# First stage of a graph network on one core: GpSimd's gathers held to four pairs ahead of VectorE's messages

## The chip, the cores and the metric

The kernel runs on one core of one Trainium2 chip. The metric is the device time of one execution in microseconds. The kernel before takes 1134.37 us, the median of three runs (1134.0 to 1136.73).

## What is computed

The reference is two graph layers over 3125 nodes and 53125 edges, the edges sorted by target node. The first layer gathers a row of `x` (256 floats) for every edge, scales it with the edge's weight, and sums over the edges of each target; the second layer adds a small network over 64 edge attributes to its messages and then puts each node through three dense layers (256 to 1024 to 1024 to 256) with layer norms.

```
messages = edge_val[:, None] * embeddings[edge_src]
neighbor_emb = segment_sum(messages, edge_dst)
out = leaky(embeddings @ W1.T + b1 + (neighbor_emb + neighbor_emb * embeddings) @ W2.T + b2)
x = layernorm(x + out / max(norm(out), eps))

e = relu(edge_attr @ ee_w1 + ee_b1) @ ee_w2 + ee_b2
h = (1 + eps) * x + segment_sum(x[src] + e, dst)
h = relu(ln(h @ w1 + b1)); h = relu(ln(h @ w2 + b2)); y = h @ w3 + b3
out = layernorm(x + relu(ln(x + y)))
```

## The kernel before, in words

Nodes are cut into 25 blocks of 128. Since edges are sorted, the edges of block q are close to a run of 17 tiles of 128 edges (the last block has 8). The tiles of a block are worked in 9 pairs: pairs 0 to 7 have two tiles, pair 8 has one (`PAIRS`). The kernel has two stages. The first stage makes, for each tile, a message in two parts (a high and a low half of float32), sums messages into target nodes by matmuls with one-hot matrices, and finishes the first layer for each block. It also sums the hidden activations of the edge network. The second stage gathers finished rows again and runs the three dense layers.

In the first stage each engine has its own written-out list of instructions, block after block; nothing but semaphores ties them together:

- GpSimd (`near_gathers`, L961) issues one indirect DMA a tile: 128 rows of `x` into `raw[:, j, :]`, where j is the tile's number in its block. `raw` has 17 places, so the gather of pair k of block q must wait until message pair k of block q-1 has read them. The semaphore `issued` counts gathers as GpSimd finishes issuing them; `gathered[j]` tells when the rows have landed.
- TensorE (`edge_layer`, L1102) multiplies the edge attributes of a pair into `ps_e` (three banks, so it waits for message pair k-2, L1106), sums tiles into `ps_sum` (`near_step`, L1118), and once a block transposes the finished sum `s_r` (`turn`, L1138), which increments `s_turned`.
- ScalarE (`highs`, L1652) writes the high halves of a pair: `raw` times the weight (L1658), and relu of `ps_e` (L1661), then increments `high`.
- VectorE (`near_block`) makes one-hots (`equal`, L216), then the low halves (L2162 and L2168); the last of them increments `message`, one for each pair. In step s of block b it works on message pair s+3 (LEAD = 3), counted on into block b+1. After the message it does a piece of the tail of an earlier block, and in step 1 `take_s` (L2173).
- SyncE loads attributes, weights and rows in its own order.

Two more ties matter. Before each pair VectorE runs `follow` (L2244), a wait that the pair's one-hot carries:

```
tiles = TILES * q + PAIRS[k][0] + 2 + AHEAD
dve.wait_ge(issued, tiles)
```

with AHEAD = 4 and TILES = 17. And from block FIRST_HELD = 4 on, GpSimd is held beyond what `raw` asks for: by HELD_PAIRS more messages, and before j = 2 by `s_turned`.

Of the kernel before, what the change touches and what calls it, by code (L numbers as in the profile page):

```python
# [48 lines left out]
assert LAST_TILES % 2 == 0  # L49
LEAD = 3  # L50
FIRST_HELD = 4
HELD_PAIRS = 3
AHEAD = 4
ENDING = 3
CHUNKS = [(0, 6), (6, 6), (12, 5)]
# [164 lines left out]
def is_last(b):  # L220

    return isinstance(b, int) and b == BLOCKS - 1
# [49 lines left out]
def gnn_program(nc, x, xT, src, dst, weight, attrT, w1T, w2T, bias01, bias02, eps_in, ee_w1, ee_b1row, ee_b1,  # L272
# [6 lines left out]
    with ExitStack() as keep:  # L279
# [29 lines left out]
        with ExitStack() as ca:  # L309
# [3 lines left out]
            def ma(name):  # L313
                return sem(name)
# [96 lines left out]
            s_turned = ma("s_turned")  # L411
# [513 lines left out]
        def _(pool):  # L925
# [35 lines left out]
            def near_gathers(q):  # L961

                for j in range(LAST_TILES if is_last(q) else TILES):
                    if j == 2 and q >= FIRST_HELD:
                        pool.wait_ge(s_turned, q - 1)
                    if j % 2 == 0:

                        pool.wait_ge(message, NP * (q - 1) + j // 2 + 1 + (HELD_PAIRS if q >= FIRST_HELD else 0))
                        pool.nop(nofuse=True)
                    pool.indirect_dma_start(  # L970
                        out=raw[:, j, :], out_offset=None, in_=x,
                        in_offset=bass.IndirectOffsetOnAxis(
                            ap=src_all[:, q * TILES + j:q * TILES + j + 1], axis=0),
                        engine_sem=issued,
                    ).then_inc(gathered[j], 16)

            def near_program(path):
                for q in range(1, BLOCKS):
                    near_gathers(q)
                second_near(path)  # L980
# [1846 lines left out]
```

## Time and profile before

| | us |
|---|---|
| median of three timed runs | 1134.37 |
| span of the profiled execution | 1477.5 |
| PE busy in it | 1201.4 |
| DVE busy | 976.8 |
| POOL busy | 812.9 |
| ACT busy | 686.1 |

For the profiled execution the span from the first to the last instruction is what is recorded; no device time of its own is given beside it. That span is 343 us longer than the median of the timed runs, so a row of the trace is not a share of the median. Engines: PE is TensorE's matmuls, PEld its weight loads, DVE VectorE, ACT ScalarE, POOL GpSimd, SP SyncE. "L970" is line 970 of the kernel. In brackets behind an instruction stands the idle time of its engine before it and what ended it; "issue" is time in which the engine waited for nothing that the profile shows, and "remote" is a release that the profile can't name. The ends of matmuls are modelled.

### The profile page before, as it was taken

To read this page: it belongs to the slowest core of one execution; us is meant where nothing else is said; L and a number is where in the kernel's file an instruction comes from. 1 tells how busy PE (TensorE), PEld (TensorE's weight loads), DVE (VectorE), ACT (ScalarE), POOL (GpSimd) and SP (SyncE) were. 2 spreads that over 40 slices of the span, in tenths; PEclk is the share of its full clock that TensorE was granted. 3 is DMA by queue.
4 is the path that set the end of the run, shared out by engine and by line. 5 is a ranking of instruction groups with operands and counts; after the bars stand their busy time and mean duration, and the time that the engine had idled before them with its cause. 6 is when DMAs were issued, how large, how long until landed. Compare 5 with 4: busy or idle time off the path is not lost.

```text
span 1477.5 us, 21215 instructions
## 1 busy us (share of the span) xinstructions
PE 1201.4 (81%) x5297; PEld 977.9 (66%) x5297; DVE 976.8 (66%) x2795; ACT 686.1 (46%) x1677; POOL 812.9 (55%) x840
## 2 busy tenths in 40 slices
PE   4788877787777887778777889888898898898897
PEld 3576666566666665566555677677776777776676
DVE  4767755667656775667666666666666676676575
ACT  2455644556445554455453443443533443443444
POOL 7555555455554555545645565566565566566530
PEclk9798887888878888788878899999999999999999
DMA  6345544445444444435565555656665566566540
GB/s 202 105 120 145 151 130 144 125 142 147 134 143 128 128 127 119 126 114 148 146 203 163 165 169 172 185 167 183 176 185 166 174 176 178 171 185 180 161 119 13
DMA packets 106088, 222.13 MB, mean 150 GB/s; under 512 B 20003, under 2 KB 57369, under 8 KB 106010
## 3 DMA queue, kind: packets, MB, share of 16 engines
q0 software_dynamic: 53408, 164.16, 39.1%
q1 hardware_dynamic: 52602, 57.11, 12.4%
q8 instruction: 27, 0.44, 0.1%
q14 instruction: 51, 0.42, 0.1%
HBM read 203.96 MB, written 17.23 MB: 150 GB/s over the span
## 4 chain that ended last, share of the span: by engine, by line
PE 34%; another core or an unknown queue 21%; DVE 16%; issue 16%; ACT 11%; DVEq 1%; DMA 1%; POOL 1%; ACTq 0%; POOLq 0%
PE ps_z L1386 8%; PE ps_e L1108 7%; PE ps_sum L1115 3%; PE ps_sum L1113 3%; ACT msg L1658 3%; ACT aF L1888 3%; PE ps_y L1386 3%; PE ps_s L1330 3%; DVE msg L2162 2%; DVE oh L216 2%; PE ps_tr L1455 2%; DVE msg L2168 2%; PE ps_w L1209 2%; ACT msg L1661 2%
## 5 line engine op out<-in xcount | busy, mean ns | idle before, releaser
L970 POOL DMA_INDIRECT raw<-in_x,src_all x399 | 385.6, 966 | 321.9 <-DVE msg L2168 177.2
L1031 POOL DMA_INDIRECT grow<-table_dram,src_all x401 | 392.7, 979 | 275.0 <-issue 115.1
L1108 PE MATMUL ps_e<-we,attr 65*128 65x256 f32 x832 | 251.1, 427 | 150.7 <-DVE msg L2168 127.0
L2162 DVE SCALAR_TENSOR_TENSOR msg<-raw,w_sb,msg 128x256 fp32r<-128x256 f32 x416 | 183.0, 478 | 242.5 <-issue 130.5
L1108 PEld LDWEIGHTS ps_e<-we,attr 65*128 65x128 f32 x832 | 171.5, 214 | 200.4 <-issue 173.3
L1661 ACT ACTIVATE msg<-ps_e 128x512 fp32r<-128x512 f32 (+1 forms) x220 | 124.3, 565 | 310.2 <-remote 221.1
L1113 PE MATMUL ps_sum<-msg,oh 128*128 128x512 f32 x464 | 255.8, 551 | 9.2 <-DVE msg L2168 8.8
L1386 PE MATMUL ps_z<-w_high,a 128*128 128x512 f32 x784 | 255.5, 395 | 7.7 <-issue 6.3
L216 DVE TENSOR_SCALAR oh<-lane,rel 128x128 fp32r<-128x128 f32 x871 | 208.1, 297 | 18.9 <-issue 15.7
L1115 PE MATMUL ps_sum<-msg,oh 128*128 128x512 f32 x464 | 210.1, 453 | 0.0
L1658 ACT ACTIVATE msg<-raw,w_sb 128x256 fp32r<-128x256 f32 x416 | 188.1, 498 | 10.3 <-issue 7.7
L1386 PEld LDWEIGHTS ps_z<-w_high,a 128*128 128x128 f32 x784 | 147.0, 188 | 40.1 <-issue 9.5
L1888 ACT ACTIVATE aF<-ps_tr,be,g 128x128 f32<-128x128 f32 x392 | 147.3, 464 | 53.7 <-PE ps_tr L1455 33.1
L1386 PE MATMUL ps_z<-w_low,a 128*128 128x512 f32 x392 | 153.4, 391 | 1.0 <-issue 0.8
L2168 DVE SCALAR_TENSOR_TENSOR msg<-ps_e,msg 128x512 fp32r<-128x512 f32 (+1 forms) x220 | 143.6, 653 | 0.0
L1455 PE MATMUL ps_tr<-ident,zn 128*128 128x128 f32 x400 | 64.3, 301 | 76.5 <-issue 38.8
L1113 PEld LDWEIGHTS ps_sum<-msg,oh 128*128 128x128 f32 x464 | 102.9, 222 | 34.0 <-issue 11.7
L1115 PEld LDWEIGHTS ps_sum<-msg,oh 128*128 128x128 f32 x464 | 104.1, 224 | 22.4
L1455 PEld LDWEIGHTS ps_tr<-ident,zn 128*128 128x128 f32 x400 | 50.1, 155 | 89.0 <-issue 88.4
L1330 PE MATMUL ps_s<-grow,oh 128*128 128x512 f32 x365 | 104.2, 429 | 0.4 <-issue 0.4
L1386 PE MATMUL ps_y<-w_high,a 128*128 128x256 f32 x400 | 89.6, 306 | 4.1 <-DVE a L2538 2.1
L1386 PEld LDWEIGHTS ps_z<-w_low,a 128*128 128x128 f32 x392 | 73.8, 188 | 18.6 <-issue 5.2
(189 smaller groups left out, 1591.6 us busy)
## 6 DMA issues: line engine op xcount, KB each, us to landing
attr<-in_attrT SPq DMA_DIRECT2D x50, 192.0 KB
raw<-in_x,src_all POOLq DMA_INDIRECT x416
grow<-table_dram,src_all POOLq DMA_INDIRECT x401
w_raw<-in_m_w SPq DMA_DIRECT2D x48, 128.0 KB
table_dram<-table SPq DMA_DIRECT2D x23, 256.0 KB
attr<-in_attrT SPq DMA_DIRECT2D x24, 160.0 KB
xs<-in_x SPq DMA_DIRECT2D x24, 128.0 KB
xTb<-in_xT SPq DMA_DIRECT2D x24, 128.0 KB
```

Of the source, the lines that this page charges most:

```text
L216: ins = dve.tensor_scalar(out_[:, i, :], lanes, which[:, i:i + 1], None, ALU.is_equal)
L970: pool.indirect_dma_start(out=raw[:, j, :], out_offset=None, in_=x, in_offset=bass.IndirectOffsetOnAxis(ap=src_all[:, q * TILES + j:q * TI ...
L1031: pool.indirect_dma_start(out=grow[:, j, :].bitcast(F32), out_offset=None, in_=table_dram, in_offset=bass.IndirectOffsetOnAxis(ap=src_all[ ...
L1108: mm = pe.matmul(ps_e[k % 3][:, (j - j0) * D:(j - j0 + 1) * D], attr[:, j * P:(j + 1) * P], we1[:, :], start=True, stop=True)
L1113: pe.matmul(ps_sum[bank][:, :], oh[:, slot, :], msg[:, j, 0, :], start=start, stop=False, skip_group_check=True)
L1115: return pe.matmul(ps_sum[bank][:, :], oh[:, slot, :], msg[:, j, 1, :], start=False, stop=stop, skip_group_check=True)
L1386: mm = pe.matmul(acc, left[a], right[b], start=False, stop=stop and a == 1, skip_group_check=True)
L1658: act.activation(msg[:, j, 0, 0:D], raw[:, j, :], ACT.Copy, scale=w_sb[:, tile_cols(n, j)])
L1661: act.activation(msg[:, j0:j0 + m, 0, D:2 * D], ps_e[k % 3][:, 0:m * D].rearrange("p (j d) -> p j d", d=D), ACT.Relu).then_inc(high, 1)
L1888: ins = act.activation(aF[layer][:, k, :], ps_tr[:, half, c * P:(c + 1) * P], ACT.Relu, bias=bb[:, k:k + 1], scale=gg[:, k:k + 1])
L2162: dve.scalar_tensor_tensor(msg[:, j, 1, 0:D], raw[:, j, :], w_sb[:, tile_cols(n, j)], msg[:, j, 0, 0:D].bitcast(F32), ALU.mult, ALU.subtract)
L2168: dve.scalar_tensor_tensor(msg[:, j0:j0 + m, 1, D:2 * D], ps_e[k % 3][:, 0:m * D].rearrange("p (j d) -> p j d", d=D), 0.0, msg[:, j0:j0 + ...
```

## The change

HELD_PAIRS goes from 3 to 5. From block 4 on the gather of pair k of block q waits for the messages up to pair k+5 of block q-1 instead of k+3, each counted on into block q where k+5 is over 8. The wait of the gather of tile 2 for the turned sum of block q-2 is taken out. Nothing else is changed.

```
-HELD_PAIRS = 3
+HELD_PAIRS = 5
...
             def near_gathers(q):

                 for j in range(LAST_TILES if is_last(q) else TILES):
-                    if j == 2 and q >= FIRST_HELD:
-                        pool.wait_ge(s_turned, q - 1)
                     if j % 2 == 0:

                         pool.wait_ge(message, NP * (q - 1) + j // 2 + 1 + (HELD_PAIRS if q >= FIRST_HELD else 0))
```

## Rows read from the trace of the kernel before

**Rows 1.** The page: busy shares, and groups of instructions with their idle time

```profile
PE 1201.4 (81%) x5297; PEld 977.9 (66%) x5297; DVE 976.8 (66%) x2795; ACT 686.1 (46%) x1677; POOL 812.9 (55%) x840
...
L970 POOL DMA_INDIRECT raw<-in_x,src_all x399 | 385.6, 966 | 321.9 <-DVE msg L2168 177.2
...
L2162 DVE SCALAR_TENSOR_TENSOR msg<-raw,w_sb,msg 128x256 fp32r<-128x256 f32 x416 | 183.0, 478 | 242.5 <-issue 130.5
```

**Rows 2.** Waits, whole span: us in total, times, longest

```profile
ACT msg L1661 <- remote: 221.1, 40, 7.9
...
PE ps_e L1108 <- DVE msg L2168: 127.0, 37, 7.6
...
ACT hT L1860 <- remote: 101.4, 21, 6.2
...
POOL raw L970 <- PE ps_t L1143: 36.5, 13, 3.9
...
DVE oh L216 <- issue: 15.7, 31, 1.2
```

**Rows 3.** Timeline of PE: start, duration, instruction

```profile
398.58 1.03 PE L1108 MATMUL ps_e<-we,attr 65*128 65x256 f32 x4
...
400.37 1.03 PE L1108 MATMUL ps_e<-we,attr 65*128 65x256 f32 x4
```

**Rows 4.** Timeline of ACT over the same stretch

```profile
404.04 0.60 ACT L1661 ACTIVATE msg<-ps_e 128x512 fp32r<-128x512 f32 x1 [3.87 <-PE ps_e L1108]
...
413.20 0.60 ACT L1661 ACTIVATE msg<-ps_e 128x512 fp32r<-128x512 f32 x1 [7.19 <-remote]
```

**Rows 5.** Timeline of POOL

```profile
393.28 0.94 POOL L970 DMA_INDIRECT raw<-in_x,src_all  x1 [2.94 <-PE ps_t L1143]
...
409.61 0.94 POOL L970 DMA_INDIRECT raw<-in_x,src_all  x1 [0.30 <-issue]
416.08 0.96 POOL L970 DMA_INDIRECT raw<-in_x,src_all  x1 [5.53 <-DVE msg L2168]
418.59 1.09 POOL L970 DMA_INDIRECT raw<-in_x,src_all  x1 [1.54 <-DVE msg L2168]
...
424.48 0.94 POOL L970 DMA_INDIRECT raw<-in_x,src_all  x1 [3.55 <-DVE msg L2168]
...
769.59 0.95 POOL L1031 DMA_INDIRECT grow<-table_dram,src_all  x1 [12.19 <-DMA table_dram<-w_high]
```

**Rows 6.** Timelines of DVE and, for turn's L1143, of PE

```profile
389.18 0.41 DVE L2181 SCALAR_TENSOR_TENSOR s_r<-xs,ps_sum 128x256 f32<-128x256 f32 x1
...
415.95 0.47 DVE L216 TENSOR_SCALAR oh<-lane,rel 128x128 fp32r<-128x128 f32 x2
...
417.13 0.68 DVE L2168 SCALAR_TENSOR_TENSOR msg<-ps_e,msg 128x512 fp32r<-128x512 f32 x1
...
419.78 0.41 DVE L2181 SCALAR_TENSOR_TENSOR s_r<-xs,ps_sum 128x256 f32<-128x256 f32 x1
...
421.63 0.68 DVE L2168 SCALAR_TENSOR_TENSOR msg<-ps_e,msg 128x512 fp32r<-128x512 f32 x1
...
422.62 0.48 DVE L216 TENSOR_SCALAR oh<-lane,rel 128x128 fp32r<-128x128 f32 x2
...
423.08 0.60 PE L1143 MATMUL ps_t<-ident,s_r 128*128 128x128 f32 x4
...
423.80 0.68 DVE L2168 SCALAR_TENSOR_TENSOR msg<-ps_e,msg 128x512 fp32r<-128x512 f32 x1
...
425.46 0.53 DVE L216 TENSOR_SCALAR oh<-lane,rel 128x128 fp32r<-128x128 f32 x2 [0.35 <-issue]
...
426.70 0.68 DVE L2168 SCALAR_TENSOR_TENSOR msg<-ps_e,msg 128x512 fp32r<-128x512 f32 x1
...
427.96 0.53 DVE L216 TENSOR_SCALAR oh<-lane,rel 128x128 fp32r<-128x128 f32 x2
...
429.21 0.53 DVE L216 TENSOR_SCALAR oh<-lane,rel 128x128 fp32r<-128x128 f32 x2
```

More of the change, by code:

```diff
@@ L51 @@
 FIRST_HELD = 4
-HELD_PAIRS = 3
+HELD_PAIRS = 5
 AHEAD = 4
@@ L963, in near_gathers @@
                 for j in range(LAST_TILES if is_last(q) else TILES):
-                    if j == 2 and q >= FIRST_HELD:
-                        pool.wait_ge(s_turned, q - 1)
                     if j % 2 == 0:
```

## The prediction

> **What bounds the kernel now.** I read four views in this order. The page's busy shares name no single engine: PE 81%, POOL 55%, DVE 66%, while POOL's first-stage gathers and DVE's messages both stand idle for hundreds of microseconds [rows 1]. So I asked who waits. The two largest sums that end in nothing the trace can name are ScalarE's: 221.1 us before `msg` L1661 in the first stage and 101.4 us before `hT` L1860 in the second [rows 2]. The timelines show what that is. TensorE starts the edge matmuls of two pairs at 398.58 and 400.37 and goes on, yet ScalarE's reads of their results start at 404.04 and 413.20 [rows 3, 4]. GpSimd meanwhile issues 14 gathers one behind the other (393.28 to 409.61), and ScalarE is let go 2.6 us after the last of them ended at 410.55 [rows 4, 5]. TensorE's completions arrive late while GpSimd gathers without a pause.
>
> That is how the profiled execution gets its 1477.5 us; the timed runs have a median of 1134.37. The two can be brought together: 1477.5 - 221.1 - 101.4 = 1155.0, within 2% of the median. A block of the first stage tells the same: `take_s` starts at 389.18 and 419.78, 30.6 us apart [rows 6]. Without the late releases VectorE needs six steps from 415.95 to 429.21, 13.26 us, or 2.2 us a step, and its other three steps at that rate make 6.7: **20.0 us a block**. GpSimd's gathers start every 1.25 us [rows 5], 17 a block: 21.25 us. If 22 blocks shrink from 30.6 to 20.0 (233 us) and the second stage loses its 101, the span is 1143; at 21.25 it would be 1170. The median is nearer to the first. So I take the timed first stage as a loop in which VectorE and GpSimd are nearly equally loaded, at 20.0 to 21.25 us a block, with next to no stall in it. The sum below is the added time of the loop; it is laid on the timed median, since the profiled span holds some 322 us that the timed runs do not have.
>
> **The change part by part.** In pairs: when VectorE has finished message pair M-1, GpSimd may now issue up to pair M+3; it was M+5.
>
> *The hold for the turned s is taken out.* It held GpSimd 36.5 us in 13 places, 2.94 us in the block shown [rows 2, 5]. By itself worth 0 to 36.5 us. But the gather it stood before (j=2, pair 1 of block q) now needs message pair 6 of block q-1. Turn's matmuls of block q-1 start at 423.08 and the gather starts at 424.48 today; that message ends at 424.48 and would let it go 0.8 us later [rows 5, 6]. The new wait is later than the old one, so I take 0.
>
> *Two pairs less of lead.* What is queued behind the longer wait is GpSimd's whole remaining list of gathers. Who waits for them is VectorE, and by a wait that the diff doesn't show: `follow` (L2244) holds pair k of block q until `issued` has reached 17q+2k+6, that is until four tiles beyond the pair are issued. For pairs 0 to 5 these tiles lie inside pair M+2, allowed one message earlier. But pair 8 has one tile instead of two. For pair 6 the last tile needed is j=0 of the next block, for pair 7 j=2, for pair 8 j=4: each time the first tile of pair **M+3**, which GpSimd may issue only when message M-1 is done. So three times a block the two engines take turns: message, wake, gather, `follow`, message. Before, that tile was allowed two messages earlier.
>
> The price of one turn: a held gather starts 0.78 us after the message that frees it (message 417.13+0.68 = 417.81, gather 418.59) and takes 0.95, after which `issued` counts: 1.73 us [rows 5, 6]. VectorE has work of its own in between, which covers part. From the end of message pair 5 (422.31) to its next one-hot (422.62) it is 0.31; after pair 6 (424.48 to 425.46) 0.98; after pair 7 (427.38 to 427.96) 0.58 [rows 6]. The waits are 1.42 + 0.75 + 1.15 = 3.3 us a block. Nothing hides them: ScalarE's `high` and TensorE's edge matmuls of later pairs wait for the same messages (L1106), and the sums too.
>
> Blocks 4 to 24 are held (FIRST_HELD = 4), so 21 wraps: 21 x 3.3 = 69 us. Against it goes what slack VectorE has in a block. It is 0 if VectorE sets the pace and 1.25 if GpSimd does; by the median I am nearer to the first and take 0.4. **21 x 2.9 = 61 us, and 1134.4 + 61 = 1195 us.**
>
> Both ends of it. Least: the wake shrinks to the 0.30 between two gathers that are not held [rows 5], the turn is 1.25, the waits 0.94 + 0.27 + 0.67 = 1.9, less the full slack 1.25: 0.6 x 21 = 13 us, 1148. Most: GpSimd sets the pace. It then has pair M+4 ready to issue 1.55 us after `follow` is satisfied (one more tile of 1.25 and 0.30), but the message takes 1.86 (422.62 to 424.48) and the wake 0.78, so GpSimd stands 1.1 us at each of three turns, and 0.9 or so once more where the row of gathers catches up: 4.2 x 21 = 88 us, 1222.
>
> On the wake the Trainium skill has another price. "Advanced Engine Details and Errata", section Network/Comms, puts the reading of a semaphore value by a sequencer at 50 to 100 ns; with the ordinary 0.30 in front of a gather that is an estimated 0.4 us, the waits 1.04 + 0.37 + 0.77 = 2.2, and the time 1134 + 21 x 1.8 = 1172. The trace has 0.78 for this very wait, two instructions deep (a wait, a nop, then the gather), and I stay with it.
>
> *The tail of the stage.* The last held gathers come up to two messages later, about 4 us. GpSimd's next work, the early gathers of the second stage, ends before a wait of 12.19 us for the stored table [rows 5], which covers it: 0. SyncE and ScalarE get no new wait, and no queue gets another transfer.
>
> **The rivals.**
>
> *Faster: the late completions are in the timed runs too.* Place: TensorE's increments while GpSimd gathers in a row. Price: 221.1 us in the profiled first stage, some 10 us a block. The change cuts the row: GpSimd can be only four pairs ahead, and stops at every message around the wrap. For it speaks that ScalarE was freed as GpSimd paused [rows 4, 5]. Against it, 1155 against 1134 leaves the timed runs hardly any of it. It decides from the point where a timed block holds over 3.3 us of late completions. With 4.5 us it would be 21 x 1.2 = 25 us faster, 1109.
>
> *The same: the turns are hidden.* TensorE is the bound by enough, and the messages are two to three pairs ahead of the sums. Then 1.0 or more of slack at each turn swallows them: 1134. For it: PE's 81% busy [rows 1]. Against it: its edge matmuls wait for message k-2 only, and 127.0 us of its idle time ends in a message [rows 2].
>
> *Partly hidden*: half the turns' price, by a shorter wake or by slack: 1134 + 13 to 1134 + 35, about 1158.
>
> *GpSimd sets the pace*: 4.2 us a block, 1222, worked out above.
>
> **How the numbers follow.** The forecast with its upper rival, 1160 to 1224: 0.61. Partly hidden, 1138 to 1160: 0.14. The same: 0.08. Faster: 0.17. A change under 0.3%, 3.4 us, is what the measurement can't tell from none. So slower is 0.75, same 0.08, faster 0.17. The likeliest case's own range is 1160 to 1222; the range that leaves out no more than 2 in 10 runs from 1128 to 1224.
>
> **What would show it.** In the changed trace GpSimd's waits for the turned s are gone, and its gathers come in groups of two around the wrap, each behind a DVE message, with 1 us and more of idle before them. DVE's one-hots L216 of pairs 6, 7 and 8 stand behind gathers, with 0.7 to 1.4 us of idle each, where today all idle time there comes to 15 us in the run. If these waits are there and the time is not longer, the slack was larger than I took. If they are not there, I have the counting of `follow` wrong. The rows of gathers are shorter, so the unnamed waits before L1661 should shrink from 221 us; the profiled span may then fall while the timed median rises. I am wrong outright if the timed median falls: the late completions would then be a cost of the timed runs too.

## The result, and the profile after

The changed kernel takes 1228.63 us (median of four, 1226.75 to 1229.07) against 1134.35 for the kernel before on the same chip: a ratio of 1.0817 with an interval of 1.0801 to 1.0832, 94 us slower. The forecast was 1195, range 1128 to 1224. The direction came out, and so did the turns that the two engines take; the size did not: 61 us forecast, 94 measured, and the time lies 4.6 us above the range. The engine taken for the pace-setter was the wrong one.

The page of the profile after (span 1224.9 us; that execution took 1226.75): busy us and share of each engine, then two groups of instructions with busy time, mean ns, and idle time before them. The first and the two groups answer to [rows 1].

```profile
PE 1103.6 (90%) x5297; PEld 904.2 (74%) x5297; DVE 983.9 (80%) x2795; ACT 690.0 (56%) x1677; POOL 805.6 (66%) x840
...
L968 POOL DMA_INDIRECT raw<-in_x,src_all x399 | 379.7, 952 | 212.1 <-DVE msg L2166 113.5
...
L2160 DVE SCALAR_TENSOR_TENSOR msg<-raw,w_sb,msg 128x256 fp32r<-128x256 f32 x416 | 181.8, 473 | 7.9 <-ACT msg L1659 7.5
```

Its waits (us in total, times, longest) answer to [rows 2]. Neither of ScalarE's "remote" waits nor the wait for the turned sum is there any more:

```profile
POOL raw L968 <- DVE msg L2166: 113.5, 105, 1.5
...
DVE oh L216 <- DMA raw<-in_x,src_all: 109.7, 129, 3.0
...
PE ps_e L1106 <- DVE msg L2166: 79.8, 74, 4.1
```

VectorE now waits 109.7 us for gathers and GpSimd 113.5 us for messages. The two timelines of one wrap show how these belong together. First VectorE, pairs 5 to 8 (start, duration, instruction; in brackets the idle time before it and what ended it), the answer to [rows 6]:

```profile
421.64 0.40 DVE L2179 SCALAR_TENSOR_TENSOR s_r<-xs,ps_sum 128x256 f32<-128x256 f32 x1
...
422.31 0.52 DVE L216 TENSOR_SCALAR oh<-lane,rel 128x128 fp32r<-128x128 f32 x2
...
423.54 0.68 DVE L2166 SCALAR_TENSOR_TENSOR msg<-ps_e,msg 128x512 fp32r<-128x512 f32 x1
...
425.97 0.53 DVE L216 TENSOR_SCALAR oh<-lane,rel 128x128 fp32r<-128x128 f32 x2 [1.35 <-DMA raw<-in_x,src_all]
...
427.21 0.68 DVE L2166 SCALAR_TENSOR_TENSOR msg<-ps_e,msg 128x512 fp32r<-128x512 f32 x1
...
429.64 0.53 DVE L216 TENSOR_SCALAR oh<-lane,rel 128x128 fp32r<-128x128 f32 x2 [1.13 <-DMA raw<-in_x,src_all]
...
433.31 0.53 DVE L216 TENSOR_SCALAR oh<-lane,rel 128x128 fp32r<-128x128 f32 x2 [1.23 <-DMA raw<-in_x,src_all]
...
437.62 0.53 DVE L216 TENSOR_SCALAR oh<-lane,rel 128x128 fp32r<-128x128 f32 x2 [0.65 <-DMA raw<-in_x,src_all]
...
446.98 0.40 DVE L2179 SCALAR_TENSOR_TENSOR s_r<-xs,ps_sum 128x256 f32<-128x256 f32 x1
```

and GpSimd over the same stretch, the answer to [rows 5]:

```profile
424.99 0.94 POOL L968 DMA_INDIRECT raw<-in_x,src_all  x1 [1.48 <-DVE msg L2166]
426.24 0.95 POOL L968 DMA_INDIRECT raw<-in_x,src_all  x1 [0.31 <-issue]
428.66 0.94 POOL L968 DMA_INDIRECT raw<-in_x,src_all  x1 [1.47 <-DVE msg L2166]
429.91 0.95 POOL L968 DMA_INDIRECT raw<-in_x,src_all  x1 [0.30 <-issue]
432.33 0.94 POOL L968 DMA_INDIRECT raw<-in_x,src_all  x1 [1.47 <-DVE msg L2166]
433.58 0.95 POOL L968 DMA_INDIRECT raw<-in_x,src_all  x1 [0.30 <-issue]
435.33 0.94 POOL L968 DMA_INDIRECT raw<-in_x,src_all  x1 [0.81 <-DVE msg L2166]
```

Read them as one chain. The message ends at 427.21 + 0.68 = 427.89; the gather it frees starts 0.77 us later (428.66) and ends at 429.60; the one-hot that `follow` held starts at 429.64; its message frees the gather at 432.33. A round takes 3.67 us, and in it GpSimd issues two gathers, which take 2.50 when nothing holds them. Hence 1.17 us more, three times a block, and 0.5 at a fourth gather (0.81 instead of 0.30). `take_s` follows after 446.98 - 421.64 = 25.34 us. The profile names the gather's transfer as what ends VectorE's waits; the wait is `follow`'s for `issued`, since the one-hot starts 0.04 us after GpSimd ends the gather, while the rows land a median of 2.8 us after their issue.

**What to compare with.** The profile shown of before was of a disturbed execution: 1477.5 us, where the timed runs take 1134. The numbers can't be understood without a second one, so the kernel before was run again (`before_again`, the first experiment). Its profiled execution took 1137.93 us, with a span of 1136.0, and its page and waits are:

```profile
PE 1082.8 (95%) x5297; PEld 895.4 (79%) x5297; DVE 986.4 (87%) x2795; ACT 687.8 (61%) x1677; POOL 802.5 (71%) x840
...
L970 POOL DMA_INDIRECT raw<-in_x,src_all x399 | 378.8, 949 | 121.6 <-issue 114.2 <-DVE msg L2168 7.3
```

```profile
POOL raw L970 <- issue: 114.2, 375, 0.3
...
DVE oh L216 <- DMA raw<-in_x,src_all: 17.5, 66, 0.6
```

GpSimd's 399 gathers have 121.6 us of idle time before them, 0.30 each, and the longest is 0.3: none is ever held, and GpSimd never stops. The timeline of VectorE has `take_s` every 21.27 us (428.67 - 407.40), which is 17 gathers of 1.25:

```profile
47.72 0.41 DVE L2181 SCALAR_TENSOR_TENSOR s_r<-xs,ps_sum 128x256 f32<-128x256 f32 x1
...
407.40 0.40 DVE L2181 SCALAR_TENSOR_TENSOR s_r<-xs,ps_sum 128x256 f32<-128x256 f32 x1
...
428.67 0.40 DVE L2181 SCALAR_TENSOR_TENSOR s_r<-xs,ps_sum 128x256 f32<-128x256 f32 x1
...
528.47 0.40 DVE L2181 SCALAR_TENSOR_TENSOR s_r<-xs,ps_sum 128x256 f32<-128x256 f32 x1
```

**Where the time went.** In the changed kernel the last `take_s` of the first stage starts at:

```profile
619.78 0.40 DVE L2179 SCALAR_TENSOR_TENSOR s_r<-xs,ps_sum 128x256 f32<-128x256 f32 x1
```

That is 91.3 us later than 528.47, and what comes behind it is 2.4 us shorter (1224.9 - 619.78 = 605.1 against 1136.0 - 528.47 = 607.5): together the 88.9 us between the two spans. The medians are 94.3 apart. All of it arises in the first stage: in the twelve later profiles the time from the last `take_s` to the end lies between 603.6 and 607.6 us whatever the kernel, so the 2.4 is no effect of the change.

### The profile page after: what moved, and what is told of

It reads as the page before. It is cut to its first block, busy times and chain, and to the rows that moved or that the text cites. A ratio compares the mean times of both kernels' runs of the same rounds, so it can differ in the third digit from the quotient of the medians.

```text
span 1224.9 us, 21215 instructions
## 1 busy us (share of the span) xinstructions
PE 1103.6 (90%) x5297; PEld 904.2 (74%) x5297; DVE 983.9 (80%) x2795; ACT 690.0 (56%) x1677; POOL 805.6 (66%) x840
## 4 chain that ended last, share of the span: by engine, by line
PE 45%; DVE 22%; issue 13%; POOL 10%; DMA 8%; ACT 1%; POOLq 0%; DVEq 0%; ACTq 0%
PE ps_z L1384 25%; POOL raw L968 9%; DVE msg L2160 8%; DMA raw<-in_x,src_all 7%; DVE msg L2166 6%; PE ps_s L1328 6%; PE ps_y L1384 5%; DVE oh L216 5%; PE ps_tr L1453 3%; PE ps_e L1106 1%; PE ps_y L1333 1%; POOL grow L1029 1%; PE ps_sum L1111 1%; PE ps_sum L1113 1%; DMA grow<-table_dram,src_all 1%
## 5 line engine op out<-in xcount | busy, mean ns | idle before, releaser
L968 POOL DMA_INDIRECT raw<-in_x,src_all x399 | 379.7, 952 | 212.1 <-DVE msg L2166 113.5
L1106 PE MATMUL ps_e<-we,attr 65*128 65x256 f32 x832 | 233.9, 404 | 81.9 <-DVE msg L2166 79.8
L216 DVE TENSOR_SCALAR oh<-lane,rel 128x128 fp32r<-128x128 f32 x871 | 209.0, 298 | 111.3 <-DMA raw<-in_x,src_all 109.7
L1106 PEld LDWEIGHTS ps_e<-we,attr 65*128 65x128 f32 x832 | 156.7, 198 | 134.3 <-issue 111.6
L1111 PE MATMUL ps_sum<-msg,oh 128*128 128x512 f32 x464 | 233.9, 504 | 7.5 <-DVE msg L2166 7.3
L1656 ACT ACTIVATE msg<-raw,w_sb 128x256 fp32r<-128x256 f32 x416 | 194.4, 499 | 57.2 <-DMA raw<-in_x,src_all 48.0
L1113 PE MATMUL ps_sum<-msg,oh 128*128 128x512 f32 x464 | 188.5, 406 | 0.0
L1111 PEld LDWEIGHTS ps_sum<-msg,oh 128*128 128x128 f32 x464 | 91.7, 198 | 34.7 <-issue 16.2
L1897 ACT ACTIVATE fm<-fm,ln_eps 128x1 f32<-128x1 f32 x50 | 14.8, 295 | 159.7 <-DVE fm L2483 159.6
L1113 PEld LDWEIGHTS ps_sum<-msg,oh 128*128 128x128 f32 x464 | 92.0, 198 | 16.9
L1328 PE MATMUL ps_s<-grow,oh 128*128 128x512 f32 x365 | 95.2, 400 | 0.4 <-DVE oh L216 0.2
L1384 PE MATMUL ps_y<-w_high,a 128*128 128x256 f32 x400 | 81.7, 288 | 2.5 <-DVE a L2536 2.3
L2478 DVE BATCH_NORM_STATS2 bs<-ps_z 128x6 f32<-128x512 f32 x100 | 69.1, 693 | 14.7 <-PE ps_z L1384 14.2
```

Source lines behind the costliest of these rows:

```text
L216: ins = dve.tensor_scalar(out_[:, i, :], lanes, which[:, i:i + 1], None, ALU.is_equal)
L968: pool.indirect_dma_start(out=raw[:, j, :], out_offset=None, in_=x, in_offset=bass.IndirectOffsetOnAxis(ap=src_all[:, q * TILES + j:q * TI ...
L1106: mm = pe.matmul(ps_e[k % 3][:, (j - j0) * D:(j - j0 + 1) * D], attr[:, j * P:(j + 1) * P], we1[:, :], start=True, stop=True)
L1111: pe.matmul(ps_sum[bank][:, :], oh[:, slot, :], msg[:, j, 0, :], start=start, stop=False, skip_group_check=True)
L1113: return pe.matmul(ps_sum[bank][:, :], oh[:, slot, :], msg[:, j, 1, :], start=False, stop=stop, skip_group_check=True)
L1328: return pe.matmul(ps_s[:, :], oh[:, slot, :], grow[:, j, :], start=start, stop=stop, skip_group_check=True)
```

## The experiments

All are measured against the kernel before, run on the same chip. Edits are given against the changed kernel, or against the kernel before where it says so.

**before_again: the kernel before once more.** No edit.

> The kernel before, unchanged, for a second profile. If the late TensorE completions are a mark of the first profiled execution only, the span is about 1133 us and a block of the first stage takes 20 to 21.3 us, with no unnamed wait before L1661 (theory). If they belong to every profiled execution of this kernel, the span is again near 1477 us and a block near 30.6 us (rival).

1135.29 against 1136.06, ratio 1.0 (0.9984 to 1.0016), span 1136.0. The profile has no "remote" wait at all, so the 322 us of unnamed waits [rows 2] belong to that one execution. It also settles which engine sets the pace, as shown above: GpSimd, at 21.25 us a block, and not VectorE at 20.0.

**lead6_noturned: only the wait for the turned sum taken out.** Against the kernel before:

```
-                    if j == 2 and q >= FIRST_HELD:
-                        pool.wait_ge(s_turned, q - 1)
```

> The removed hold for the turned s alone, the lead as before (six pairs). Theory of the turns (the cost is the three take-turns of message, gather and follow at the end of each block): within 0.3% of before, 1131 to 1138 us. Rival (the hold for the turned s kept GpSimd's gathers apart from the other engines' work, and its loss is part of the 94 us): 1150 us or more.

1136.06 against 1136.06, ratio 1.0007 (0.9991 to 1.0023). This half of the change does nothing that can be measured.

**lead4_turned: only the shorter lead.** Against the kernel before:

```
-HELD_PAIRS = 3
+HELD_PAIRS = 5
```

> The shorter lead alone (four pairs), with the hold for the turned s kept. Theory of the turns: all of the loss, 1225 to 1232 us, since that hold is over before the message that now frees the gather. Rival: clearly below 1220 us, if the hold has a share.

1226.24 against 1136.06, ratio 1.0804 (1.0779 to 1.0829). This half does everything: the interval overlaps that of the whole change. VectorE waits 110.0 us for gathers, against 109.7 in the changed kernel.

**lead5_noturned: one pair less instead of two.**

```
-HELD_PAIRS = 5
+HELD_PAIRS = 4
```

> HELD_PAIRS = 4, a lead of five pairs, no hold for the turned s. Theory of the turns: the tile that follow asks for is freed one message earlier, no turn is left, and the time is that of before within 0.3%, 1131 to 1139 us. Rival (the loss grows with the pairs of lead taken away): half of 94 us, about 1180 us.

1136.87 against 1135.20, ratio 1.001 (0.9996 to 1.0025). GpSimd's waits come back to 0.30 each, but for one of 1.4 us and one of 0.6. The cost has a threshold between five pairs and four: with five, GpSimd may always issue a whole pair beyond what `follow` asks for, and with four it may not.

**no_hold: no hold at all.** Against the kernel before:

```
-FIRST_HELD = 4
+FIRST_HELD = 99
```

> The kernel before with FIRST_HELD = 99: no hold at all beyond what the raw rows ask for, and none for the turned s. The second profile of before shows no pause between any two of the first stage's gathers, so no hold is ever reached. Theory: 1133 to 1138 us, the same as before. Rival (the holds keep a bad phase away): over 1139 us.

1135.79 against 1136.37, ratio 0.9991 (0.998 to 1.0001). The hold of the kernel before is never reached, neither to its cost nor to its profit.

**lead4_ahead2: the changed kernel, and `follow` asks for two tiles less.**

```
-AHEAD = 4
+AHEAD = 2
```

> The changed kernel with AHEAD = 2 instead of 4 in follow, so that VectorE asks for two tiles beyond its pair and not four; GpSimd's holds are as in the changed kernel. Theory of the turns: no tile that follow asks for is the one that the last message frees, so the turns are gone and the time is 1130 to 1145 us. Rival (it is the short lead as such: rows land too late, or GpSimd is paused too often): still 1200 us or more, with the waits now at ScalarE's L1656 for the gathered rows.

1162.18 against 1136.06, ratio 1.0233 (1.0211 to 1.0255). That `follow` is one of the two parties is shown: 68 of the 94 us go. But 1130 to 1145 was expected, and 26 us stay. The group of the gathers:

```profile
L968 POOL DMA_INDIRECT raw<-in_x,src_all x399 | 393.8, 987 | 132.1 <-issue 107.1 <-DVE msg L2166 25.1
```

10.5 us are added idle time of GpSimd (132.1 against the 121.6 of before_again), most of it before gathers still held, and 15 are in the gathers themselves (393.8 against 378.8). Is that the lead, or `AHEAD` by itself? So the next one.

**lead6_ahead2: the kernel before, and `follow` asks for two tiles less.** The same edit of AHEAD, against the kernel before.

> The kernel before with AHEAD = 2 instead of 4. lead4_ahead2 was 26 us slower than before although only 10.6 us of it was GpSimd waiting; its gathers took 0.986 us in the mean instead of 0.946. If that comes from VectorE's instructions falling into GpSimd's gathers when follow lets them start earlier, it is here too, without any hold: 1140 to 1155 us, with gathers of 0.96 us and more (theory). If it comes from the short lead, this kernel is at 1134 to 1138 us (rival).

1149.37 against 1136.37, ratio 1.011 (1.009 to 1.0129). No gather is held but one (0.8 us), yet it is 13 us slower, and the group of gathers says why:

```profile
L970 POOL DMA_INDIRECT raw<-in_x,src_all x399 | 394.0, 988 | 122.1 <-issue 104.8 <-DVE msg L2168 16.0 <-PE ps_t L1143 1.2
```

The idle time is unchanged (122.1), the gathers themselves are 15 us longer than 378.8, and on a chain that runs through every gather this is the whole loss. In the kernel before, `follow` releases VectorE as a gather ends, so that VectorE's order of work stands at a fixed place against the gathers: between 90 and 510 us, 353 of 376 one-hots start in the 0.30 us between two gathers; with AHEAD = 2 it is 134 of 363. In the same stretch 85 gathers of the second kernel take 1.0 us or more, and no gather of the first does.

The overlap alone is not the cause: the 85 overlap the messages L2162 for 0.52 us each and the 240 shorter ones for 0.28, but those of the kernel before do it for 0.39 us without harm. The trace shows more: what goes with the long gathers is when such an instruction starts, and which one it is. These messages read two operands from SBUF (`raw` and `msg`), and so do three instructions of the tail (`y`, `tb` and `table`). With AHEAD = 2, 46 gathers have one of the four starting 0.05 to 0.25 us before them, and 44 of these take 1.0 us or more; 47 gathers have another VectorE instruction starting there, with at most one tensor in SBUF (for 25 of them L2168, which reads `ps_e` from PSUM), and none of these does. In lead4_ahead2 it is 49 of 52 against none of 60. In the kernel before none of the four ever starts there. One-hots are left out of this count: they have one operand, and where they start 0.07 to 0.09 us before a gather, 25 of 38 gathers take 1.00 to 1.03 us. Why they do, and why nothing is lost when a message starts later in a gather, is open.

The Trainium skill, "SBUF — State Buffer", section "Who interferes with whom", says that a VectorE instruction with two SBUF inputs takes its second through a read path that it shares with GpSimd, and contends there with a GpSimd instruction that reads SBUF. The counts of the four agree with it. The same section infers that the making of a DMA's descriptors needs the write side, which a second input does not take; by that these gathers would go unharmed, which they do not. They also read their row numbers (`src_all`) from SBUF, and no run separates the two.

**lead4_follow_less: `follow` asks for one tile less, at the three pairs in question only.**

```
-                tiles = TILES * q + PAIRS[k][0] + 2 + AHEAD
+                tiles = TILES * q + PAIRS[k][0] + 2 + AHEAD - (1 if k >= 6 else 0)
```

> The changed kernel, with follow asking for one tile less before pairs 6, 7 and 8 only (17 tiles beyond pair 6's block start instead of 18, and so on), so that the tile it asks for is never in the pair that the last message frees. Everything else, the lead of four pairs too, is as in the changed kernel. Theory of the turns: they are gone, and GpSimd's gathers are nearly without pause: 1134 to 1150 us. Rival (a lead of four pairs costs as such): 1160 us or more, as 1162 for AHEAD = 2 would then mean.

1173.01 against 1135.20, ratio 1.0322 (1.0299 to 1.0345). A miss: 56 us go, 38 stay. The timeline of GpSimd has one held gather a block left, the first of the next block:

```profile
410.49 0.95 POOL L968 DMA_INDIRECT raw<-in_x,src_all  x1 [0.30 <-issue]
412.91 1.23 POOL L968 DMA_INDIRECT raw<-in_x,src_all  x1 [1.48 <-DVE msg L2166]
```

It waits for message pair 5, and the edit had left pair 5 alone. `follow` lets VectorE begin pair 5 when tile 15 is issued. GpSimd is then allowed only tile 16, the single tile of pair 8, 1.25 us of work, while VectorE needs 1.92 (425.97 to 427.89 in the changed kernel) and the wake 0.77. I had counted the turns from VectorE's side, where pairs 6 to 8 wait; from GpSimd's side the same turns hang on the messages 5 to 7. 21 x 1.17 = 25 us of the 38 are this wait, 6 are other gaps (the group of the gathers has 152.5 us of idle time, 30.9 over before_again), and 6 are gathers that got longer (384.7 us against 378.8). These 6 are the held gather itself, which takes 1.23 us in 20 of the blocks, as above: a message with two SBUF operands starts 0.07 us before it.

```profile
412.84 0.87 DVE L2160 SCALAR_TENSOR_TENSOR msg<-raw,w_sb,msg 128x256 fp32r<-128x256 f32 x2
```

**lead4_nonop: the wake made shorter.** The empty instruction between the wait and the gather is taken out of `near_gathers`.

```
-                        pool.nop(nofuse=True)
```

> The changed kernel without the nop between GpSimd's wait and the gather in the first stage. If the nop is a share of the 0.78 us of the wake, each of three turns a block is shorter by that share; 0.3 us less would be 21 x 3 x 0.3 = 19 us, 1210 us (theory: the price is the wake). If the wake's length is the gather's own way to GpSimd's cores, nothing changes, 1226 to 1230 us (rival).

1181.28 against 1135.20, ratio 1.0406 (1.0382 to 1.0429): 46 us above before instead of 94, half the cost of the change, for one instruction that does nothing. The timelines of GpSimd and of VectorE:

```profile
397.29 0.94 POOL L967 DMA_INDIRECT raw<-in_x,src_all  x1 [0.97 <-DVE msg L2165]
398.54 0.95 POOL L967 DMA_INDIRECT raw<-in_x,src_all  x1 [0.30 <-issue]
400.46 0.94 POOL L967 DMA_INDIRECT raw<-in_x,src_all  x1 [0.97 <-DVE msg L2165]
```

```profile
396.34 0.68 DVE L2165 SCALAR_TENSOR_TENSOR msg<-ps_e,msg 128x512 fp32r<-128x512 f32 x1
...
398.27 0.53 DVE L216 TENSOR_SCALAR oh<-lane,rel 128x128 fp32r<-128x128 f32 x2 [0.86 <-DMA raw<-in_x,src_all]
```

The held gather starts 0.27 us after the message's end (397.02 to 397.29), where it was 0.77. So the nop costs 0.50 us at each wake, and a round is 3.17 us (397.29 to 400.46) instead of 3.67. That moves the time as the turns say: 0.50 less at three turns, and the fourth wait gone, make 0.50 x 3 + 0.5 = 2.0 a block, and 21 blocks 42 us, of the 47 measured; part of the rest is that the longer gaps told of below shrink too. I had expected 1210, since I took the wake as mostly not the nop.

**lead4_from14: the short lead from block 14 on.**

```
-FIRST_HELD = 4
+FIRST_HELD = 14
```

> The changed kernel with FIRST_HELD = 14: the shorter lead holds only in blocks 14 to 24, 11 wraps instead of 21. Theory of the turns: the loss goes with the wraps, 11 x 4.1 = 45 us and 1 to 3 for the longer wakes: 1180 to 1184 us. Rival (one slow start-up or the end of the stage has a large share): well off the middle between 1136 and 1228.

1181.90 against 1135.20, ratio 1.0411 (1.0386 to 1.0437). Eleven blocks instead of 21 cost 46.7 us, 4.2 a block, and 21 cost 94.3, 4.5 a block. In its trace the blocks are 21.26 us long before the hold sets in and 25.3 after it, but for two with a longer gap (told of below). The cost is one of each held block, not of starting or ending the stage.

**lead5_ahead6: the wrong distance made at the other end.** One pair less of lead, which cost nothing, and `follow` two tiles further.

```
-HELD_PAIRS = 5
-AHEAD = 4
+HELD_PAIRS = 4
+AHEAD = 6
```

> A lead of five pairs (HELD_PAIRS = 4, 1137 us by itself) with AHEAD = 6 in follow, no hold for the turned s. The lead is a pair longer than in the changed kernel, but follow asks for two tiles more, so that from pair 5 to pair 8 the tile it asks for is again the one that the last message frees: four turns a block. Theory of the turns: as slow as the changed kernel or slower, 21 x 5 us over before, 1230 to 1250 us, with GpSimd standing before j = 0, 2, 4, 6. Rival (a short lead is what costs): faster than the changed kernel's 1228 us, near 1137.

1253.38 against 1136.37, ratio 1.1031 (1.1004 to 1.1058), 3 us above what was expected. The turns are back, with the same gap before the gather, and there are more of them a block (four whole ones and part of a fifth):

```profile
304.17 0.94 POOL L968 DMA_INDIRECT raw<-in_x,src_all  x1 [1.47 <-DVE msg L2166]
...
307.84 0.95 POOL L968 DMA_INDIRECT raw<-in_x,src_all  x1 [1.48 <-DVE msg L2166]
```

The lead of five pairs is not bad by itself: HELD_PAIRS = 4 with AHEAD = 4 is free, with AHEAD = 6 it is the slowest kernel here. (AHEAD = 6 with the lead of six pairs was not run.) What counts is the distance between the two. No version beats the kernel before: in it GpSimd issues gathers without a gap, and that is the length of the stage.

## Why the prediction was right in kind and wrong in size

*The hold for the turned sum, 0:* right (lead6_noturned, and lead4_turned against the changed kernel).

*The turns.* Right in place and number. The one-hots of pairs 6, 7 and 8 wait 1.35, 1.13 and 1.23 us; the prediction had 1.42, 0.75 and 1.15. The 0.75 was misread from the rows: of the 0.98 us after pair 6's message that it took for VectorE's own work, 0.35 are idle time, which stands in brackets behind 425.46 [rows 6]; without them it is 1.10. `follow` is the partner (lead4_ahead2, lead4_follow_less, lead5_ahead6), and the turn begins with the one-tile pair, as argued. That pair 6's message frees j=2 and not an earlier gather was right too; what I did not draw out is the same count for GpSimd, and it cost the expectation of lead4_follow_less.

*The wake, 0.78:* right, 0.77 in the changed kernel. The wake of 0.4 that was estimated from the Trainium skill, "Advanced Engine Details and Errata", section Network/Comms, and its 1172 stood against it. The trace disagrees as long as the nop is there; without it the whole wake is 0.27, and 0.50 of the 0.77 is the nop, which the price of reading a semaphore does not count.

*The tail, 0:* right. The second stage is as long as before, within what the runs differ by.

*The late completions.* That "the profiled span may then fall while the timed median rises" is what happened, 1477.5 to 1224.9 and 1134 to 1229, though not because the changed kernel has shorter rows of gathers: the kernel before falls to 1136.0 by itself. The rival "faster" is refuted: no profile of an execution of the usual length has its 221 us. The rivals "the same" and "partly hidden" fall with the 94 us.

*The step that failed* is "The median is nearer to the first. So I take the timed first stage as a loop in which VectorE and GpSimd are nearly equally loaded, at 20.0 to 21.25 us a block", and from it "I am nearer to the first and take 0.4" for the slack. The block takes 21.25 us, GpSimd sets the pace, and the forecast's pace-setter was the wrong engine. The argument was a subtraction from the disturbed span: 233 us for the blocks and 101 for the second stage, which gave 1143 and seemed to speak for 20.0. Both terms were off. From the first `take_s` to the last the difference is 199 us. The start, 18 us later in the disturbed execution, had been left out (this row stands against 47.72 above):

```profile
65.67 0.41 DVE L2181 SCALAR_TENSOR_TENSOR s_r<-xs,ps_sum 128x256 f32<-128x256 f32 x1
```

And the second stage lost 125 us and not 101. The last `take_s` of the two:

```profile
745.29 0.42 DVE L2181 SCALAR_TENSOR_TENSOR s_r<-xs,ps_sum 128x256 f32<-128x256 f32 x1 [2.67 <-remote]
```

(1477.5 - 745.29) - 607.5 = 125. So 18 + 199 + 125 = 342, the whole difference of the spans. The two paces are 27 us apart in such a sum (22 blocks of 1.25), and its terms were off by 34, 18 and 24: it could not tell them apart.

*The term of the sum.* The prediction priced the turns by VectorE's waits less its slack, 2.9 us a block. GpSimd has no slack, and what is lost is what GpSimd stands still. Measured: 1.17 three times and 0.5 once, a block of 25.33 us against 21.25, **4.08 more**, 21 x 4.08 = 86 us. VectorE's own books come to the same, if they are kept in full: it stands idle 0.94 us in the block of before_again from 407.40 to 428.67, and 5.13 in the block shown of the changed kernel, 4.2 more. What the forecast's 2.9 lacks there is, for the most part, the misread 0.35 and the wait of 0.65 at a fourth one-hot (437.62, above), where GpSimd's row of gathers is behind; the forecast put that at nothing, since it took VectorE for the pace-setter and GpSimd for an engine that catches up. GpSimd's idle time in the group of gathers says the same: 212.1 - 121.6 = 90.5 us, the longer gaps told of below among it. This is the rival "GpSimd sets the pace" with its 4.2 us, 88 and 1222; it had been worked out with the right mechanism and given too little weight. That its sum is so near is in part luck: 1.1 at each of three turns was 1.17, and 0.9 once more was 0.5.

*What the range missed.* Between these 86 us and the 91.3 of the stage lie some 5 us. The changed kernel has five gaps of GpSimd that are longer than the pattern, at gathers 113, 208, 210, 307 and 404 of the stage, counted from 0; they are 1.8 or 1.9 us long but for one of 3.2. The four blocks that hold them are 1.5, 2.6, 0.4 and 1.5 us longer than the others, 6.1 together, and the prediction has no term for them. Two of the gaps, in the timeline of GpSimd:

```profile
303.35 0.95 POOL L968 DMA_INDIRECT raw<-in_x,src_all  x1 [1.76 <-issue]
...
308.73 0.94 POOL L968 DMA_INDIRECT raw<-in_x,src_all  x1 [3.19 <-issue]
```

They fall on the same gathers in lead4_turned, so they are not chance. They are not a fixed cost of a place in the program either: the kernel before and no_hold, whose lists for GpSimd differ from those of lead4_turned and the changed kernel only in the counts waited for, have no gap over 0.3 us there, and lead4_from14 has only the two that lie in its held blocks. (The two longer gaps of lead5_noturned, 1.4 and 0.6 us, are at 210 and 307.) Nor are they wakes that take longer, since three of the five (113, 307 and 404) stand before a gather that has no wait. What they are, the trace doesn't say, and no run took them apart. The last 5 us, from the spans' 88.9 to the medians' 94.3, are the choice of execution: the profiled one of the changed kernel is 1.9 us under its median (1226.75 against 1228.63), and that of before_again 3.6 us over 1134.35 (1137.93).

## What to carry to other kernels

When one engine may run at most so far ahead of another, and the other asks for a minimum lead of the first, work out the room between the two limits in the smallest unit, and across the odd-sized one at a wrap: with one tile of room the engines take turns, wake and all, and with a pair of room both limits were free here. In such a loop ask first which engine has no gap between its instructions, since a wait costs what that engine stands still, whatever slack the other has. And when a profiled execution is 343 us longer than the median, don't infer the pace of a loop from differences of its sums: take a second profile, or give both readings equal weight.

## What the runs showed of the hardware

- An empty instruction between a wait and an indirect gather on GpSimd costs 0.50 us of a wake of 0.77 (lead4_nonop). In the rows of gathers of before_again, none of them held, nothing shows of it: 0.30 between two, with a wait and nop before every other one.
- The pitch of gathers that are not held is 0.95 + 0.30 = 1.25 us, in the 1136 us kernels as in those of 1229. Where VectorE starts an instruction with two SBUF operands 0.05 to 0.25 us before a gather, the gather takes 1.0 us or more instead of 0.95: 44 of 46 in lead6_ahead2, 49 of 52 in lead4_ahead2, and 20 of 20 in lead4_follow_less, at 1.23 us. With what else got longer the mean is 988 ns in lead6_ahead2, which is 13 us of this kernel.
- In one execution ScalarE's waits for what TensorE had computed lasted up to 7.9 us and ended in releases that the profile can't name [rows 2]; that execution is 342 us longer than the next one. None of the twelve later profiles told of here (the changed kernel and eleven runs) has such a wait.
- In the changed kernel GpSimd has gaps of 1.8 to 3.2 us before five gathers, with a wait before them or without, and the same ones in lead4_turned; before the same gathers the kernel before has 0.30. The cause is open.
